# Where VectorE computes the gated product among the softmax maxima of an even step

## The reference

```python
def ffn(x):                                   # D = 512, H = 2048
    gate, up = split(x @ ternary_quant(w_gate_up).T)
    h = silu(gate) * up
    return rms_norm(h) @ ternary_quant(w_proj).T

def attention(x):                             # 32 heads of 16, blocks of 128 tokens
    q, k, v = heads(x @ Wq.T), heads(x @ Wk.T), heads(x @ Wv.T)
    scores = q @ [previous block's k, own k].T / sqrt(16)     # 128 x 256 for a head and block
    scores = where(0 <= dist <= 128 and the key exists, scores, min)
    return (softmax(scores) @ [previous v, own v]) @ Wo.T

x = x + 0.5 * ffn(layernorm(x))               # A
x = x + attention(layernorm(x))               # B
x = x + 0.5 * ffn(layernorm(x))               # C
```

## Time and profile before

| | us |
|---|---|
| median of 3 runs | 2010.4 |
| lowest, highest | 2005.5, 2012.08 |
| the profiled execution | 2012.65 |
| its span from the first to the last instruction | 2010.5 |

### The profile page before, as it was taken

One profiled execution on the slowest core, in us unless ns is written; L12 is line 12 of the kernel. 1 busy time (PEld: TensorE's weight loads), 2 busy tenths in 40 slices (PEclk: granted clock), 3 DMA queues, 4 the chain that ended last, 5 costly groups with the idle time before them and its releaser, 6 DMA issues.

```text
span 2010.5 us, 37842 instructions
## 1 busy us (share of the span) xinstructions
PE 1890.9 (94%) x12501; PEld 918.3 (46%) x12744; DVE 1550.5 (77%) x4080; ACT 1499.0 (75%) x2870; POOL 572.6 (28%) x560
## 2 busy tenths in 40 slices
PE   6677899999999999999999999999999999999868
PEld 3353344444444444444444444444444444444334
DVE  8966787778787878777887878777887787777763
ACT  6937778777776878777877787778777777778662
POOL 2012223323332323223333232323332333322210
PEclk8889999999999999999999999999999999999999
DMA  6326788779897898879886998879887888878862
GB/s 227 130 58 111 143 141 166 134 141 159 158 155 116 149 161 153 142 139 158 151 152 127 155 155 158 145 137 155 154 147 133 153 153 156 152 124 151 143 117 63
DMA packets 1031618, 287.58 MB, mean 143 GB/s; under 512 B 1016064, under 2 KB 1017088, under 8 KB 1030912
## 3 DMA queue, kind: packets, MB, share of 16 engines
q1 hardware_dynamic: 1031424, 285.15, 78.3%
HBM read 25.17 MB, written 8.39 MB: 17 GB/s over the span
## 4 chain that ended last, share of the span: by engine, by line
PE 79%; issue 2%; DVE 2%; DMA 1%; ACT 1%; SPq 1%; POOL 0%; DVEq 0%; POOLq 0%; ACTq 0%
PE ps_gu L1127 38%; PE ps_yy L1193 20%; PE ps_om L1173 14%; PE ps_om L1205 4%; PE ps_s L1183 2%; DMA ht<-hh 1%; PE ps_yy L1183 1%; SPq L439 1%; DVE prob L917 1%; DVE masked L943 1%; ACT masked L791 0%; DMA kt<-k 0%; ACT prob L806 0%; DVE hid L932 0%; DVE hh L917 0%
## 5 line engine op out<-in xcount | busy, mean ns | idle before, releaser
L791 ACT ACTIVATE masked<-masked,exp_bias,exp_scale 128x256 f32<-128x256 f32 (+1 forms) x1024 | 503.7, 562 | 8.8
L1193 PE MATMUL ps_yy<-wp_t,ht 128*128 128x512 bf16 x1977 | 478.5, 384 | 28.3 <-DMA ht<-hh 26.1
L1127 PE MATMUL ps_gu<-wgu_t,xt_A 128*128 128x512 bf16 x1943 | 466.7, 381 | 10.1 <-DVE hid L926 2.5
L1127 PE MATMUL ps_gu<-wgu_t,xt_C 128*128 128x512 bf16 x1931 | 459.8, 379 | 7.7 <-DVE v L921 1.9
L917 DVE TENSOR_TENSOR prob<-masked,prob 128x1024 f16<-128x1024 f32 (+1 forms) x256 | 284.4, 1111 | 45.6 <-ACT prob L806 45.1
L1193 PEld LDWEIGHTS ps_yy<-wp_t,ht 128*128 128x128 f16 x2008 | 187.6, 99 | 262.2 <-issue 31.9
L932 DVE SCALAR_TENSOR_TENSOR hid<-ps_gu,h_scale_u,hid 128x512 f32<-128x512 f32 x252 | 189.2, 751 | 147.8 <-PE ps_gu L1127 142.1
L663 ACT ACTIVATE hh<-hid 128x512 f16<-128x512 f32 x256 | 160.8, 628 | 182.9 <-DVE hid L932 175.8
L587 POOL TENSOR_TENSOR xh<-xhat,xh 128x512 f16<-128x512 f32 x94 | 109.8, 1168 | 649.3 <-ACT xh L663 649.3
L1127 PEld LDWEIGHTS ps_gu<-wgu_t,xt_A 128*128 128x128 f16 x2048 | 191.7, 98 | 221.6 <-issue 7.8
L1127 PEld LDWEIGHTS ps_gu<-wgu_t,xt_C 128*128 128x128 f16 x2032 | 189.2, 97 | 214.2 <-issue 3.7
(11 more groups left out here) (177 smaller groups left out, 2276.7 us busy)
## 6 DMA issues: line engine op xcount, KB each, us to landing
stream<-in_L_attn_x_dram SPq DMA_DIRECT2D x32, 256.0 KB, 3.0
pt<-prob SPq DMA_TRANSPOSE x512, 3.3
out_dram<-stream SPq DMA_DIRECT2D x32, 256.0 KB, 2.6
prob<-in_L_ffn_w_gate_up_dram SPq DMA_DIRECT2D x4, 1024.0 KB, 6.3
ht<-hh SPq DMA_TRANSPOSE x255, 3.2
stream<-in_L_ffn_w_gate_up_dram SPq DMA_DIRECT2D x3, 1024.0 KB, 5.4
stream<-in_L_ffn_w_proj_dram SPq DMA_DIRECT2D x2, 1024.0 KB, 4.9
prob<-in_L_ffn_w_proj_dram SPq DMA_DIRECT2D x2, 1024.0 KB, 4.8
```

The source lines that it names most:

```text
L791: t = act.activation(p, p, ACT.Exp, bias=exp_bias[:, 4 * g + h:4 * g + h + 1], scale=exp_scale[:, 0:1])
L1127: t = pe.matmul(bank[:, :], xt[s][:, part, k, :], wgu_t[:, k, at:at + CH], start=(k == 0 and part == 0), stop=(k == KD - 1 and part == 1))
L1193: t = pe.matmul(ps_y[:, :], ht[:, n % HRING, i, :], wp_t[:, 4 * c + i % 4, :], start=(c == 0 and i == 0), stop=(c == NC - 1 and i == 2 * N ...
```

## The change

In an even step VectorE takes the maxima of group g, then computes the gated product of this step's quarter, then takes the maxima of group g + 1. Before, the product came behind both. The branch for the step `LAST_WO`, which stood between the maxima and the product, now stands behind the first group's maxima; that step has no scores. Nothing else is changed.

```diff
@@ -1047,7 +1047,6 @@
                 b, g = group_at(step, SCORES)
                 if b is not None and g % 2 == 0:
                     masked_max(b, g)
-                    masked_max(b, g + 1)
                 if step == LAST_WO:
                     add_output(LAST, ps_m)
                     norm_stats("C", LAST, d_x2, NB)
@@ -1055,6 +1054,9 @@
                 s, bf, c, n = gate_at(step)
                 if s:
                     gated(s, bf, c, n)
+                b, g = group_at(step, SCORES)
+                if b is not None and g % 2 == 0:
+                    masked_max(b, g + 1)
 
                 b = summed("A", step)
                 if b is not None:
```

## The result

The changed kernel takes 2026.91 us (median of four runs, 2022.88 to 2027.55), the kernel before, measured beside it, 2008.79 (2005.5 to 2012.08). The ratio, with its 95% interval, is 1.0079 [1.0066, 1.0093]: slower by 15.9 us, 13.3 to 18.7. The profiled run took 2027.06 us, 14.4 more than the profiled run before (2012.65).

A forecast was written before the change was run, and what follows sets the result against it. TensorE was taken to bound the kernel, every steady pause being lost. Wo 11.9, waiting K 2.4 and the other Q, K and V 3.9 sum to 18.2 us; 2010.4 + 18.2 = 2028.6 us, range 2021 to 2036 (80%).

The forecast's parts named there:

- What bounds the kernel: Steady stage: TensorE busy 396.35 of 400 us, so every pause of it is lost and freeing only VectorE gains nothing.
- The product: Gated product on VectorE ends four maxima earlier; next gate matmuls gain 0 to 0.7 us, taken as 0.
- The slot: On VectorE, the second group's maxima end later by one product's slot, 0.60 us.
- The rival with the maxima behind the product's end: VectorE: maxima start only once the product has ended, 0.68 or 0.79 us later; 2035.0 or 2043.8 us; chance 6%.
- Wo, steady: Wo projections into ps_m have no slack: 18 lose 0.60 us each, three others 1.1 together; 11.9 us in all.
- The three partial ones: Three Wo projections already some 0.16 to 0.32 us late for another reason lose less than 0.60 each, 1.1 us together.
- Q, K and V: 53 steady Q, K and V projections lose 3.1 us; one late K 0.41 and one late V 0.33; sum 3.9 us.
- The rival by which the steady ones pay nothing: Q, K and V have Wo's latency, so only Wo and waiting K pay: 15.0 us, 2025.4; chance 22%.
- K already waiting: Four K projections (188, 240, 298 and 1894 us) already waiting for row_max lose 0.60 us each, 2.4 us.
- The sum: Whole kernel: 11.9 + 2.4 + 3.9 = 18.2 us more, giving 2028.6 us.
- The pause paid once: TensorE falls back 0.60 us once, not in each block: 3.0 us, 2013.4; chance 6%.
- The clock: Gaps lower TensorE's clock, each Wo step running the rest of its matmuls slower: 54 us, 2083; chance 2%.

The follow-up runs named there:

- run 2: Kernel before, with the change's order in all even steps except those ending in a Wo projection: 2014.53 us, ratio 1.0018.
- run 3: Changed kernel, but the second group's two maxima reading ps_m go first and the projection waits for those alone: 2009.0 us, ratio 0.9995.
- run 10: Kernel before, with the product between the second group's ps_m maxima and its last two, the projection waiting for the ps_m pair alone: 2008.78 us, 0.9994.
- run 1: Kernel before, with the change's order only in the even steps that end in a Wo projection: 2021.28 us, ratio 1.0051.
- run 4: Kernel before, second group's ps_m maxima first and the projection waiting for those alone, run twice: 2008.21 us (0.9989) and 2008.76 us (0.9992).
- run 6: Changed kernel plus one unused 512-column maximum on VectorE between the product and the second group: 2077.89 us, ratio 1.0342.
- run 7: Kernel before, with the product moved ahead of both groups' maxima: 2052.96 us, ratio 1.0219.
- run 9: Kernel before, ps_m maxima ahead of all others, projection waiting for those alone, then first group, then the other two: 2015.89 us, ratio 1.0038.

## Why the prediction was right, and where its sizes were off

Forecast were 2028.6 us, 18.2 more than before; measured are 2026.91, 15.9 more (13.3 to 18.7).

*What bounds the kernel.* Right. Pauses of TensorE go through to the span, but for what run 2 leaves open, and run 3 (0.9985 to 1.0005) shows that nothing else in the change costs or gains anything that can be measured.

*The product.* Right: gain 0. Runs 3 and 10, both with an earlier product, stand at 0.9995 and 0.9994.

*The slot.* 0.60 us forecast, 0.60 measured (1019.88 to 1020.48). The rival with the maxima behind the product's end falls with it, and so does the 1.10 that the prediction estimated by the Trainium skill, VectorE: DVE Perf Modes, "The DRAIN you can't avoid". It had left out the end of that paragraph, "A next op that is not held starts earlier", by which the page need not ask for 1.10 here; the trace agrees with it, 0.60 behind an operation of 0.68.

*Wo, steady.* Right in kind, 0.025 us too large in size. All 17 undisturbed ones lose 0.57 to 0.58. The term that was a little off is "the slack is nil": in the kernel before, TensorE's matmul started 0.080 us after the last readout's end, while it starts 0.058 after it when it really waits (from the rows above, rounded: 1022.00 less 1021.86 and 0.08). There were 0.02 us to spare. The one at 270 us, which waited already, loses 0.597. The three partial ones lose 0.41, 0.32 and 0.25, together 0.98 where 1.1 was forecast. All of Wo: 17 x 0.575 + 0.60 + 0.98 = 11.36 us, forecast 11.9. The group behind short maxima starts in its cadence, as forecast.

*Q, K and V.* Right. The 53 steady ones lose 0.05 to 0.07 each, 3.12 us together, and the late K and V 0.41 and 0.33: 3.86, forecast 3.9. The rival by which the steady ones pay nothing falls by the traces of the change and of run 2, in which every one of them is late. The times can't tell it from the forecast: its 15.0 us lie in the change's interval too, and in run 2 it would leave 3.1 us of the waiting K and the two late ones, where the ratio stands for 3.6. The traces also show which latency holds: 0.147 us from the readout's end to the matmul in these, 0.058 in Wo.

*K already waiting.* Right. The pause of each of the four is 0.60 longer, that of the one at 240 us with its wait up from 1.02 to 1.62 us:

```profile
241.18 1.02 PE L1175 MATMUL ps_om<-wk,xt_B 128*128 128x512 f16 x4 [1.62 <-DVE row_max L943]
```

*The sum.* By its terms as they are in the trace it would be 11.36 for Wo, 2.40 for the waiting K and 3.86 for Q, K and V: 17.6 us, where 18.2 was forecast. The profiled runs differ by 14.4. Where do the other 3 lie? In the steady stage, 13.48 stand against 14.5 by its terms; behind it, from the last steady K to the last Wo projection, the changed kernel is 0.6 us later by the fourth waiting K and gets 2.2 earlier elsewhere, in shorter waits for transposes. I read those as scatter and not as an effect of the change: run 2 has that K 0.60 later too and keeps it (0.55 later over the same stretch), and runs 1 and 3, whose K has no longer pause, are 0.78 and 0.42 later there. In the steady stage, a wait of the kernel before,

```profile
613.12 1.24 PE L1173 MATMUL ps_om<-wo,ot 128*128 128x512 f16 x5 [1.28 <-issue]
```

which is shorter after,

```profile
618.43 1.89 PE L1175 MATMUL ps_om<-wo,ot 128*128 128x512 f16 x8 [1.04 <-issue]
```

is absent in runs 1 and 3, and another is not there before:

```profile
1439.51 1.69 PE L1175 MATMUL ps_om<-wq,xt_B 128*128 128x512 f16 x7 [0.63 <-DMA xt_B<-xh]
```

It stands in runs 1 to 4 too, whatever their order, and in none of the others. How far single profiled runs can differ with no cause in the order is seen on one kernel in the two of run 4: 2007.79 and 2010.13 us. So a difference of 3 us between two traces of different orders isn't evidence for or against the terms, though that it is scatter isn't shown either. The ratio over all runs, 15.9 us (13.3 to 18.7), holds both 17.6 and 18.2 and is what the terms should be judged by.

*The pause paid once.* Falls. VectorE waits 0.92 us for TensorE in the Wo step of after as of before, and every undisturbed Wo is late anew. The sign put down for it, that VectorE's waits for TensorE grow by the whole sum, came true in part: those ahead of the product with ps_u went from 142.1 to 143.1 us, those of the attention's normalisation (L953) from 82.2 to 89.1. VectorE's waits for ScalarE's tanh grew too, from 54.5 to 62.6, all of the growth in steps whose product isn't moved: no moved product waits for it, as forecast.

*The clock.* The steady stage has 1.00 in both kernels, so it stays at the upper level with a pause of 0.57 us in each block; run 6, with 1.01 us ahead of Wo and 0.5 ahead of Q and K, shows 1.00 too in the window from 310 to 1890 us:

```profile
310.00:1890.00 1580.00, 1518.86 (x10011) 714.47 (x10210) 1267.50 (x3417) 1177.97 (x2317) 493.59 (x455) 1.00 0.80 142
```

The up and down of the clock that the Trainium skill, TensorE: Matmul & The Clock Gate, "A second HAM failure mode: psum-queue depth-cycling", tells of is not seen with these pauses.

## What to carry to other kernels

Before moving work on an engine that is not the bottleneck, find who waits for what it is moved past, and measure the slack of each from the end of the last instruction needed to the start of the one that needs it, in every kind of step; a wait that shows only as idle time of the weight loader, as that of Wo here, can be one that has used its slack up. Ask then in which order the results free what the bottleneck needs next: here that order, and not the place of the product, was worth the 0.8%. Operations moved forward also meet their inputs earlier, as the product met the tanh in run 7, and an order that frees the bank still earlier can cost more than it gives, as in run 9.

## What the runs showed of the hardware

A matmul that waited for a readout of VectorE starts 0.058 us after the readout's end in Wo, where the profile names row_max as what released the weight load, and 0.147 in Q, K and V, where the load is not held by it and the wait sits ahead of it. That the place of the wait makes the difference is likely, but no run moves it. A weight load that is late costs the matmuls nothing at first: the one at 1013.07 waited 0.31 us in the earlier trace rows, and its matmul stood in the cadence.

Between two operations of VectorE that need nothing of each other, the next starts some 0.08 us before the end of the one ahead: 0.60 behind one of 0.68, 0.34 behind one of 0.42.
